# Expert layer: 1024 middle tokens routed into 23 sorted 128-row tiles run behind the recurrence, the other 1024 tokens dense in three chunks

## The reference

```python
xw = jnp.einsum('ntd,dh->nth', x, Wx) + b
def step(prev_h, xw_t):
    next_h = jnp.tanh(xw_t + prev_h @ Wh)          # 128 steps, one after the other
    return (next_h, next_h)
...
router_logits = jnp.einsum('bth,eh->bte', x, router_w)
topk_values, topk_indices = jax.lax.top_k(router_logits, TOP_K)      # TOP_K = 2 of 8
topk_weights = jax.nn.softmax(topk_values.astype(jnp.float32), axis=-1).astype(x.dtype)
h1 = jnp.einsum('bth,efh->btef', x, w1) + b1                          # f: 512
h1 = jax.nn.gelu(h1, approximate=False)
expert_outputs = jnp.einsum('btef,ehf->bteh', h1, w2) + b2
topk_expert_outputs = jnp.take_along_axis(expert_outputs, gather_idx, axis=2)
mixed_output = jnp.sum(topk_expert_outputs * topk_weights[..., None], axis=2)
...
x = x + _L1_ffn_ref(_L1_cond_ref(x, cond_1024, ...), ...)
```

## Time and profile before

| what | us |
|---|---|
| median of 3 runs (301.9 to 303.03) | 301.91 |
| profiled execution, from first to last instruction (its span) | 301.2 |
| PE busy | 264.4 (88%) |
| DVE busy | 258.8 (86%) |
| ACT busy | 215.6 (72%) |
| POOL busy | 76.2 (25%) |

### The profile page before, as it was taken

How to read it: one execution, slowest core, us unless ns; L and a number is a source line. 1 busy time by engine, 2 the same in 40 slices (tenths; PEclk the granted TensorE clock), 3 DMA queues, 4 the chain that set the end, 5 groups by cost and what they waited for, 6 DMA issues and landing times.

```text
span 301.2 us, 8834 instructions
## 1 busy us (share of the span) xinstructions
PE 264.4 (88%) x2716; PEld 205.5 (68%) x2716; DVE 258.8 (86%) x635; ACT 215.6 (72%) x455; POOL 76.2 (25%) x148
## 2 busy tenths in 40 slices
PE   4969940049989999999999999999999999999994
PEld 4824440016956777778888788888777887888874
DVE  4888999989898897779988799887799988889885
ACT  6367899998842677767777676667566766689892
POOL 3367997000025413011302112212110311101000
PEclk9989976557999999999999999999999999999999
DMA  6990443101500000000000000000001000001000
GB/s 186 314 310 4 84 94 76 28 0 35 90 17 2 0 3 1 0 2 2 19 0 0 2 3 26 2 0 0 1 2 30 8 0 0 2 1 37 0 2 27
DMA packets 24031, 10.63 MB, mean 35 GB/s; under 512 B 13355, under 2 KB 22982, under 8 KB 24006
## 3 DMA queue, kind: packets, MB, share of 16 engines
q1 hardware_dynamic: 23470, 10.05, 13.6%
q10 hardware_dynamic: 536, 0.26, 0.3%
HBM read 6.11 MB, written 1.05 MB: 24 GB/s over the span
## 4 chain that ended last, share of the span: by engine, by line
PE 79%; DVE 16%; issue 1%; ACT 1%; DMA 1%; SPq 0%; DVEq 0%
PE bank L893 78%; DVE peak L706 3%; DVE big L728 3%; DVE peak L633 2%; DVE big L711 1%; DVE big L744 1%; PE bank L937 1%; DMA y_sb<-in_cond 1%; PE bank L1017 0%; DVE big L746 0%; DVE wyT L779 0%; DVE pkm L626 0%; DVE big L738 0%; DVE x_sb L759 0%; DVE q L700 0%
## 5 line engine op out<-in xcount | busy, mean ns | idle before, releaser
L893 PE MATMUL bank<-big,wt 128*128 128x384 f16 (+2 forms) x480 | 124.8, 336 | 0.6 <-DVE big L872 0.5
L893 PE MATMUL bank<-wt,big 128*128 (+1 forms) x1536 | 111.5, 219 | 0.1
L872 DVE TENSOR_TENSOR big<-big 128x384 f16<-128x384 f32 (+2 forms) x160 | 93.2, 585 | 20.5 <-ACT big L594 16.1
L893 PEld LDWEIGHTS bank<-wt,big 128*128 128x128 f16 x1536 | 97.9, 97 | 16.2 <-issue 0.2
L592 ACT ACTIVATE big<-bank,miscT 128x384 f32<-128x384 f32 (+2 forms) x160 | 96.2, 602 | 15.3 <-PE bank L893 8.2
L893 PEld LDWEIGHTS bank<-q,wxh 128*128 128x128 f32 x254 | 44.4, 189 | 17.4 <-issue 3.4
L893 PEld LDWEIGHTS bank<-big,wt 128*128 (+1 forms) x480 | 50.0, 117 | 4.8 <-issue 1.1
L580 ACT ACTIVATE q<-bank (+1 forms) x112 | 20.6, 184 | 38.7 <-PE bank L893 37.9
L404 POOL CAST big<-q 128x64 f16<-128x64 f32 x32 | 13.2, 413 | 129.0 <-ACT q L580 126.5
L868 DVE CAST big<-big 128x512 f16<-128x512 f32 (+2 forms) x104 | 38.6, 372 | 4.8 <-ACT big L592 3.9
L827 DVE SCALAR_TENSOR_TENSOR wyT<-bank,gates,wyT 128x128 f32<-128x128 f32 x128 | 39.8, 343 | 1.0 <-issue 0.6
(11 more groups left out here) (165 smaller groups left out, 320.0 us busy)
## 6 DMA issues: line engine op xcount, KB each, us to landing
wnat<-in_w SPq DMA_DIRECT2D x8, 512.0 KB, 7.7
x_sb<-in_x SPq DMA_DIRECT2D x4, 256.0 KB, 4.3
out_block<-wyT SPq DMA_DIRECT2D x15, 64.0 KB
wn<-in_w_gate ACTq DMA_DIRECT2D x1, 192.0 KB, 4.9
wn<-in_w_up SPq DMA_DIRECT2D x1, 192.0 KB, 5.6
wn<-in_w_down SPq DMA_DIRECT2D x1, 192.0 KB, 5.7
b_in<-in_b SPq DMA_DIRECT2D x12, 4.0 KB
wt<-wyT SPq DMA_TRANSPOSE x8, 3.0
```

The source lines that it names most:

```text
L872: V.tensor_tensor(g_lo[:, par, f, 0:w], g32[:, f, 0:w], g_hi[:, par, f, 0:w], ALU.subtract).then_inc(g_lo_done, 1)
L893: return nc.tensor.matmul(o, l, r, start=start, stop=stop, skip_group_check=True)
```

## The change

The tokens are no longer all treated alike. Tokens 0 to 255, 256 to 767 and 1792 to 2047 are three dense chunks as before (256, 512 and 256 wide). The 1024 tokens from 768 to 1791 are **routed**: each token is put twice into a table in HBM (`xs_rows`), once for each of its two experts, sorted by expert, each expert's part rounded up to whole tiles of 128 rows. At most 2 x 8 + 7 = 23 tiles come of it, and 23 are always run.

- **Recurrence.** Chunk 0 (256 wide) carries one step in each slot, 32 in all; chunk 1 (512 wide, its four pairs now written out and not looped) carries two in each slot, 64 in all. The last 16 steps run by themselves in a new function `between`, ahead of chunk 2.
- **Routing.** `between` also makes the 1024 tokens' logits, their two best experts, each row's place (a cumulative count by matmuls with a triangle of ones, then some small DVE operations), copies of the tokens with tokens as rows (matmuls by the identity, eight ACT copies of 512 columns) and the table of tiles `m_tile` (expert and first row of each tile). The logits of chunk 2 wait for that table on PE.
- **Table.** SP writes 10112 rows of zeros (544 B each, 5.5 MB) to HBM behind the weight transposes, and two rows of `b2` behind that. POOL issues 16 indirect DMAs of 128 rows (`L588`), then splits chunk 2's gates.
- **Sparse tiles.** Behind chunk 2 each of the 23 tiles: SP reads its first row from `m_tile` into a register, loads the tile transposed from HBM and the rows' return addresses; PE reads the expert into a register and makes 12 hidden matmuls, and, two tiles later, one for the bias `b2` and 12 down matmuls, 128 columns each; ACT reads the expert too and makes four gelus; DVE makes high and low halves and takes the output from PSUM; POOL scatters it to a second table in HBM by an indirect DMA.
- **End.** When all 23 have landed, SP loads both rows of every token back, DVE adds them with their gates (16 operations), and the 8 tiles are stored.

```diff
-RNN_SLOTS = ((0, 1, 3, 4, 5, 7), range(8), range(8), (0, 1, 2, 4, 5, 6), ())
-RNN_FROM = [FIRST_STEPS + E // 2 * sum(len(n) for n in RNN_SLOTS[:c]) for c in range(CH)]
-HI_SCALAR = ((3,), (3,), (3,), (3,), (0, 1, 3))
+D_WIDTHS = (256, 512, 256)
+D_FROM = (0, 256, 1792)
+DCH = len(D_WIDTHS)
+D_TILES = [w // P for w in D_WIDTHS]
+D_BEFORE = [sum(D_TILES[:c]) for c in range(DCH + 1)]
+HI_SCALAR = ((3,), (), (0, 1, 3))
+RNN_PER_SLOT = (1, 2, 0)
+RNN_FROM = (FIRST_STEPS, FIRST_STEPS + 32, T - 16)
+RNN_REFILL = 32
+TAIL_STEPS = 16
+SP_FROM = 768
+SP = 1024
+SP_TILES = SP // P
+SP_TILE0 = SP_FROM // P
+NT = 2 * SP_TILES + E - 1
+XROW = 272
+XROWS = (E - 1) * SP + NT * P
+DUMP = NT * P
+YROWS = DUMP + 2 * SP
...
-        def chunks(eng, pair):
-            for c in range(CH):
-                pair(c, 0, c > 0)
-                with eng.Fori(1, E // 2 - (c == CH - 1)) as e2:
-                    pair(c, e2, True)
-            pair(CH - 1, E // 2 - 1, True)
+        def chunks(eng, pair, between):
+            pair(0, 0, False)
+            with eng.Fori(1, E // 2) as e2:
+                pair(0, e2, True)
+            for e2 in range(E // 2):
+                pair(1, e2, True)
+            between()
+            pair(2, 0, True)
+            with eng.Fori(1, E // 2 - 1) as e2:
+                pair(2, e2, True)
+            pair(2, E // 2 - 1, True)
...
-        def rnn_step(c, e2, s):
-            if s not in RNN_SLOTS[c]:
-                return None
-            return e2 * len(RNN_SLOTS[c]) + (RNN_FROM[c] + RNN_SLOTS[c].index(s))
-        def rnn_column(c, step):
-            return (step + -RNN_FROM[c]) * B
...
+        def rnn_steps(c, e2, s):
+            n = RNN_PER_SLOT[c]
+            return [e2 * (2 * NF * n) + (RNN_FROM[c] + n * s + i) for i in range(n)]
+        def rnn_column(c, e2, step):
+            return (step + -(RNN_FROM[c] + (RNN_REFILL if c == 1 and e2 >= 2 else 0))) * B
...
+            sp.wait_ge(s_consts, 1)
+            sp.dma_start(xs_rows.rearrange("(k p) r -> p k r", p=P),
+                         zrow[:, :].unsqueeze(1).to_broadcast([P, XROWS // P, XROW])).then_inc(xs_init, 16)
+            sp.wait_ge(b2r_zeroed, 1)
+            for row in (0, BH_LO):
+                sp.dma_start(b2r_in[row:row + 1, :], b2.rearrange("(a e) h -> a (e h)", a=1)).then_inc(ld_b2r, 16)
...
+            for i in range(2 * SP_TILES // 4):
+                sp.wait_ge(sent, 16 * 4 * (i + 1))
+            sp.wait_ge(m_done, 2)
+            for n in range(NT):
+                row = sp.value_load(m_tile[0:1, 1, n:n + 1], min_val=0, max_val=XROWS - P)
+                if n >= XBUF:
+                    sp.wait_ge(s_hid, NF * (n - XBUF + 1))
+                sp.dma_start_transpose(xs_in[:, n % XBUF, :, :], xs_rows[bass.ds(row, P), 0:2 * P]).then_inc(xs_ld[n % XBUF], 16)
+                if n >= 2 * XBUF:
+                    sp.wait_ge(spot_done, n - 2 * XBUF + 1)
+                sp.dma_start(back[:, 2 * n:2 * n + 2], xs_rows[bass.ds(row, P), 2 * P:2 * P + 2]).then_inc(
+                    back_ld[n % (2 * XBUF)], 16)
...
+            for i in range(4):
+                sp.wait_ge(y_sent[i], 16 * ((NT - i + 3) // 4))
+            back_rows = ys_rows[DUMP:YROWS, :].rearrange("(a j p) h -> p j a h", a=2, p=P)
+            for j in range(SP_TILES):
+                sp.dma_start(y_back[:, j, :, :], back_rows[:, j, :, :]).then_inc(y_in[j], 16)
+            for j in range(0, SP_TILES, 2):
+                sp.wait_ge(y_added, j + 1)
+                store(nc.sync, SP_TILE0 + j).then_inc(stored, 16)
...
+            for i in range(done, T // 4):
+                split_states(i)
+            pool.wait_ge(xs_init, 16)
+            pool.wait_ge(s_consts, 6)
+            pool.wait_ge(s_pos_done, 1)
+            for j in range(SP_TILES):
+                for a in range(2):
+                    pool.wait_ge(pay_done, j // 2 * 2 + a + 1)
+                    G.indirect_dma_start(out=xs_rows, out_offset=bass.IndirectOffsetOnAxis(ap=s_pos[:, a, j:j + 1], axis=0),
+                                         in_=payload[:, j, a, :], in_offset=None).then_inc(sent, 16)
+            split_gates(DCH - 1)
+            for n in range(NT):
+                pool.wait_ge(back_ld[n % (2 * XBUF)], 16 * (n // (2 * XBUF) + 1))
+                if n >= 4:
+                    pool.wait_ge(y_sent[n % 4], 16 * (n // 4))
+                G.tensor_scalar(spot[:, n % 4:n % 4 + 1], back[:, 2 * n:2 * n + 2].bitcast(F32), dump[:, n:n + 1], 0.0, ALU.max,
+                                ALU.add).then_inc(spot_done, 1)
+                pool.wait_ge(spot_done, n + 1)
+                pool.wait_ge(s_y_sb, n + 1)
+                G.indirect_dma_start(out=ys_rows, out_offset=bass.IndirectOffsetOnAxis(ap=spot[:, n % 4:n % 4 + 1].bitcast(U32), axis=0),
+                                     in_=y_st[:, n % 4, :], in_offset=None).then_inc(y_sent[n % 4], 16)
...
+            def take_payload(i):
+                j, a = i // 2 * 2, i % 2
+                act.wait_ge(pay_mm, j + 2)
+                A(payload[:, j:j + 2, a, 0:2 * P], banks[4 + j // 2][:, :].rearrange("p (j r) -> p j r", j=2),
+                  ACT.Copy).then_inc(pay_done, 1)
+            def between():
+                for k in range(TAIL_STEPS):
+                    step = T - TAIL_STEPS + k
+                    act.wait_ge(rnn_mm, step + 1)
+                    A(h32[:, step * B:(step + 1) * B], ps_rnn[:, k * B:(k + 1) * B], ACT.Tanh, scale=1 / WS).then_inc(h32_done, 1)
+                    if 5 <= k < 5 + SP_TILES:
...
+            for n in range(NT):
+                e = act.value_load(m_tile[0:1, 0, n:n + 1], min_val=0, max_val=E - 1)
+                for f in range(NF):
+                    act.wait_ge(s_hid, NF * n + f + 1)
+                    if n >= 2:
+                        act.wait_ge(s_lo, 2 * (n - 2) + f // 2 + 1)
+                    A(s_g32[:, n % 2, P * f:P * (f + 1)], hid_of(NF * n + f), ACT.Gelu,
+                      bias=miscT[:, bass.ds(e * NF + f, 1)], scale=1 / WS).then_inc(s_gelu, 1)
...
+            def take_y(n):
+                dve.wait_ge(s_y_mm, n + 1)
+                if n >= 4:
+                    dve.wait_ge(y_sent[n % 4], 16 * (n // 4))
+                V.tensor_copy(y_st[:, n % 4, :], ps_y[n % 2][:, 0:P]).then_inc(s_y_sb, 1)
+            for n in range(NT):
+                for half in range(2):
+                    dve.wait_ge(s_gelu, NF * n + 2 * half + 2)
+                    if n >= 3:
+                        dve.wait_ge(s_y_mm, n - 2)
+                    at = slice(2 * P * half, 2 * P * (half + 1))
+                    link(V.tensor_copy(s_ghi[:, n % 3, at], s_g32[:, n % 2, at]))
+                    V.tensor_tensor(s_glo[:, n % 3, at], s_g32[:, n % 2, at], s_ghi[:, n % 3, at], ALU.subtract).then_inc(s_lo, 1)
+                if n >= 3:
+                    take_y(n - 3)
+            for n in range(NT - 3, NT):
+                take_y(n)
+            dve.wait_ge(s_gate_done, 2)
+            for j in range(SP_TILES):
+                dve.wait_ge(y_in[j], 16)
+                a = acc[:, SP_TILE0 + j, :]
+                link(V.scalar_tensor_tensor(a, y_back[:, j, 0, :], s_gate[:, 0, j:j + 1], a, ALU.mult, ALU.add))
+                V.scalar_tensor_tensor(a, y_back[:, j, 1, :], s_gate[:, 1, j:j + 1], a, ALU.mult, ALU.add).then_inc(y_added, 1)
...
+                if c == DCH - 1:
+                    pe.wait_ge(m_done, 2)
...
+            def between():
+                pe.wait_ge(h32_done, T - TAIL_STEPS)
+                input_part(T - TAIL_STEPS, T)
+                for k in range(TAIL_STEPS):
+                    step = T - TAIL_STEPS + k
+                    pe.wait_ge(h32_done, step)
...
+            def sparse_up(n, e):
+                pe.wait_ge(xs_ld[n % XBUF], 16 * (n // XBUF + 1))
+                x_hi, x_lo = (xs_in[:, n % XBUF, low, :] for low in range(2))
+                for f in range(NF):
+                    w_hi, w_lo = (wt_flat[:, bass.ds(e * (4 * FF) + (low * FF + f * P), P)] for low in range(2))
+                    slot = NF * n + f
+                    if slot == HID_BANKS.index(3):
+                        pe.wait_ge(b2_added, DCH)
+                    if slot >= len(HID_BANKS):
+                        pe.wait_ge(s_gelu, slot - len(HID_BANKS) + 1)
+                    o = hid_of(slot)
+                    mm(o, w_hi, x_hi, True)
+                    mm(o, w_lo, x_hi, False)
+                    mm(o, w_hi, x_lo, False).then_inc(s_hid, 1)
+            def sparse_down(n, e):
+                if n < 2:
+                    pe.wait_ge(added, LATE + E * D_BEFORE[DCH])
+                else:
+                    pe.wait_ge(s_y_sb, n - 1)
+                o = ps_y[n % 2][:, 0:P]
+                mm(o, ones[:, 0:P], b2_rows[:, bass.ds(e * P, P)], True)
+                for f in range(NF):
+                    w_hi, w_lo = (wt_flat[:, bass.ds(e * (4 * FF) + (2 * FF + low * FF + f * P), P)] for low in range(2))
```

(17 more changed lines are left out.)

327 lines of the change are left out of this document (247 added, 80 removed).

## The result

The changed kernel takes 326.41 us (median of 4 runs, 325.08 to 328.33) where the kernel before takes 302.0 us (4 runs): a ratio of 1.079, 95% interval 1.076 to 1.083. It is slower, as forecast, by 24.4 us in place of the 18 forecast. Its profiled execution has a span of 325.0 us. The kernel before was run again beside each set of experiments, with medians from 302.0 to 302.8 us; a ratio is to the runs of its own set, and a difference in us across sets is uncertain by about 0.8.

The account below looks back on a forecast made before the run. PE's matmuls were taken to bound the kernel; about 93 us of pairs leave, 23 sparse tiles paced by PE's sequencer come. Terms from chunk 0's logits at 103.5 sum to 319.3, plus 0.7: 320.0 us, range 303 to 343.

Parts of the forecast that it names:

- Chunk 0: First dense chunk, 256 wide: 30.7 us before plus 2.9 for 8 more recurrence steps, 33.6, ending at 137.1.
- Zeroing the table: SP's 5.5 MB zeroing, with POOL waiting for the `b2` rows behind it: costs nothing unless the rate is under 110 GB/s.
- Chunk 1: 512-wide chunk, modelled on the earlier chunk 2 (47.5 us) plus 32 steps, second refill and a wait: 53.7, ending at 190.8.
- the recurrence can't take two steps a slot: Rival for chunk 1: slots take 2.03 us, not 1.65, 12 us more, 332; chance 0.07.
- Between: Lone steps at 0.67 us, refill, logits, copies, last state and wait for the table of tiles: 17.3 us, ending at 208.1.
- Chunk 2: Last dense chunk, 256 wide, no steps: ACT sets 0.825 us a slot; 26.0 us with last down products, ending at 234.1.
- Sparse tiles: 23 tiles behind chunk 2, paced by PE's sequencer (computed addresses, register load) at 3.1 us each: 71.3 us, ending at 305.4.
- address work costs nothing: Rival for sparse tiles: PE's address work runs ahead, DVE paces at 1.8 us a tile, 41 for 71.3, 290; chance 0.10.
- The register load is dear: Rival for sparse tiles: a load costs near a DMA's 1.7 us, PE 4.2 a tile, 25 us more, 345; chance 0.13.
- SP 2.4: SP's work per sparse tile: load 0.6, transpose 1.23 and DMA 0.60, 2.4 us, under PE's 3.1.
- The late scatters: Rival in chunk 2: POOL's 16 scatters run slow, gates come 8 us late, 328, or 337 if casts block them; chance 0.13.
- The end: After the last matmul: copy, scatter, landing, eight loads, additions and last store, 13.9 us where 3.7 remained before.

Follow-up runs that it names:

- the kernels with constants: Changed kernel with sparse tiles' weight addresses constant on PE: 319.69 us, ratio 1.056; with ACT's bias and SP's rows constant too: 301.26 us, ratio 0.997.
- the rows come later: Changed kernel with POOL's clearing, loading and splitting of the `b2` rows moved behind chunk 1's gates: 322.2 us, ratio 1.063.
- the kernel with the loads ahead: Changed kernel with `b2` rows later, chunks 0 and 2 written out, PE's and SP's register loads made before the sparse tiles: 303.15 us, ratio 1.002.

## Why the prediction was right, and where it was off

The forecast was 320.0 us, slower, with PE's sequencer as the cause. The time is 326.4, inside the range, and the cause is shown by the kernels with constants. Behind the largest term, which held, smaller errors cancelled. Term by term, in the profiled execution, whose span is 1.4 us under the median where the sum allowed 0.7:

| term | forecast | measured | ends at |
|---|---|---|---|
| up to chunk 0's logits | 103.5 | 104.3 | 104.3 |
| chunk 0 | 33.6 | 38.6 | 143.0 |
| chunk 1 | 53.7 | 50.5 | 193.5 |
| between | 17.3 | 17.6 | 211.1 |
| chunk 2 | 26.0 | 27.0 | 238.1 |
| sparse tiles | 71.3 | 71.0 | 309.1 |
| end | 13.9 | 15.9 | 325.0 |

**Chunk 0** is the mis-sized term, and the step that failed in it is the sentence under "Zeroing the table": POOL's work on the `b2` rows was priced by what POOL itself is late for, at nothing. It blocks DVE, which was on the path in the first pair: 3.5 us. I had quoted the Trainium skill on the shared ports, but only for the case in which DVE locks POOL out; the same section ("SBUF — State Buffer", "SBUF: two separate sides") says it for the other direction. Of the 0.8 us ahead of the chunk 0.5 go with it (103.8 where the rows come later): the `memset` of the rows, 0.95 from 102.87, stands beside a cast that took 0.82 where it takes 0.28. (Across all the traces this mark stands between 101.9 and 104.3, so the other 0.3 says nothing.) The rest, 35.1 - 33.6 = 1.5, is mostly the price of a slot with a step in the loop: I had 1.085, and eight slots of the changed kernel's loop take 9.13 us (122.92 to 132.05), 1.14 each, which for 24 slots is 1.3 more.

**Chunk 1** came in 3.2 us shorter. Its slots are 1.65 us apart as summed, but the sum counted two slots too many. Its model, chunk 2 of before, was measured from logits to logits, and the copy of the logits comes when the third slot begins: two slots of the next chunk are in the 47.5. Here the chunk ends where the refill for the lone steps begins (193.53), and from the copy at 142.96 only 30 slots remain: 53.7 - 2 x 1.65 = 50.4. The second refill left no gap: PE is busy 50.50 of 50.50 us. With that, the rival that the recurrence can't take two steps a slot is false.

**Between** held to 0.3 us, but by luck. A lone step took 0.67 us as summed only at first (PE in order of time):

```profile
194.65 0.40 PE L1149 MATMUL bank<-q,wxh 128*128 128x16 f32 x2 [0.27 <-ACT q L772]
195.32 0.40 PE L1149 MATMUL bank<-q,wxh 128*128 128x16 f32 x2 [0.27 <-ACT q L772]
...
205.57 0.59 PE L1149 MATMUL bank<-q,wxh 128*128 128x16 f32 x2
206.43 0.61 PE L1149 MATMUL bank<-q,wxh 128*128 128x16 f32 x2 [0.27 <-ACT q L772]
```

Once PE was down to single steps with a wait in each, its granted clock fell to 0.50 (1.2 GHz) at about 197.8 and stayed there until about 214.9. From 198.5 on a step takes 0.88, with one of ACT's copies behind its tanh or without: the last one above has none and takes 0.86. So the 0.2 a copy of the sum, 1.6 us, is wrong, the copies fit beside PE's part of the step, and some 1.9 us of slower clock, of which the sum had nothing, stand in its place. PE waited 0.83 us for the table (`m_tile`, L1105) where 1.8 was in the sum.

**Chunk 2** came within 1.0 us, by luck too. Its first slots ran at the lower clock: from the logits to the slot at 215.31, 2.4 slots took 4.2 us. The slot at 211.87 took 1.92 us, where a slot with the same products, with the clock at 1.00 (the kernel with the loads ahead, 201.31), took 0.99. The other 28 took 20.0 us, 0.72 each and not 0.825, since ACT doesn't set the pace. The 0.825 added up durations, but ACT's gelus overlap too (ACT in order of time):

```profile
228.22 0.47 ACT L750 ACTIVATE big<-bank,miscT 128x256 f32<-128x256 f32 x1
228.58 0.48 ACT L752 ACTIVATE big<-bank,miscT 128x256 f16<-128x256 f32 x1
```

They start 0.36 apart, so seven of them take 2.5 us in four slots, 0.63 a slot, under PE's 0.66; PE was busy 5.00 of 5.00 us from 225 to 230. Behind the last slot 2.7 us pass until the first tile, where the sum had 1.7: the last down products, and 0.57 of "issue" ahead of the first tile.

**Sparse tiles**: 3.05 us against 3.1. The load was entered as 0.6 + 0.2 and costs 0.7 to 0.8, of which the load itself is 0.31 and the rest the gaps; the addresses 2.3 against 2.2. The rival "address work costs nothing" is false, and of the next limit it is half right: without register work the pace is 1.97, not far from its 1.8, but with POOL's queue nearest to a limit and not DVE, and the time 301, not 290. "The register load is dear" is false: 0.31 where 1.7 was feared, and the gaps make it 0.8. "SP 2.4" was wrong, 2.77, without effect on the time, as PE was later still.

**The late scatters** did not come true, by 0.7 us: a scatter is 0.97 at best and 1.27 at most beside DVE's work in chunk 2, and one that ran across a cast (the cast at 224.18, the scatter from 223.75) took 0.97. The wait of 2.5 that the forecast took from the Trainium skill's example isn't seen in any of the 16. The same section of the Trainium skill ("SBUF: two separate sides") ends the block with the VectorE instruction. A cast here is 0.29 us long, so the example's length should not have been carried over. The same ports did their damage elsewhere.

**The end** took 2.0 us more. The last tiles have no up products between them, so their y comes faster than POOL can scatter it (POOL, in order of time):

```profile
307.04 1.06 POOL L599 DMA_INDIRECT ys_rows<-wnat,spot  x1 [1.39 <-DVE wnat L1124]
...
312.06 1.05 POOL L599 DMA_INDIRECT ys_rows<-wnat,spot  x1 [0.28 <-POOL spot L595]
```

The last y is copied by 309.4 and its scatter starts at 312.06, behind two others 1.67 apart in POOL's queue. The sum had let it start at once. These 2.7 us of backlog, less 0.7 by which the other terms of the end came in shorter, are the 2.0; that is read from the trace, and no kernel was made to try it.

The balance of the change: 64 pairs of tile and expert, 93 us by the forecast's rate, leave; 71 us of sparse tiles come, and with the lone steps, a narrow chunk whose first slots run at the lower clock and the way back through memory the saving is gone before chunk 0's 5 us.

## What to carry to other kernels

Price a step on an idle engine also by whom it shares something with: a POOL instruction of 1 to 2 us can cost a cast or a two-input instruction of DVE beside it nearly its whole length, so it belongs where DVE has slack. When work becomes small per address (128 columns a matmul), count the addresses and register loads of PE's queue, not the columns: here 2.3 us of address work and 0.8 of load stand against 1.6 us in which the array does the same products without them. Loads into registers can go ahead, to a stretch with room for them, if they are done by the time their engine is needed: SP's 23 took 14 us, and PE then waited 1.8 us for its first tile. A short loop over narrow tiles (256 columns here) was worth writing out, one over 384 columns or more was not. And take an engine's pace from the distance between starts, not from durations, on ACT as on PE.

## What the runs showed of the hardware

- A POOL instruction can hold DVE's casts and two-input instructions up until it ends: 0.29 became 2.02 us, 0.15 became 0.99, beside POOL's TENSOR_TENSOR on a single partition (2.11 us) and TENSOR_SCALAR on 33 (1.09 us); few partitions didn't help.
- A register load from SBUF takes 0.28 us on SP and 0.31 on PE. With the check and the register work behind it SP made one every 0.6 us, and from its start until PE multiplied again it was 1.0, of which the array stood idle for 0.6 to 0.8.
- A scatter of 128 rows by indirect DMA holds POOL for 0.97 us (544-byte rows) or 1.06 (512-byte rows), with 0.3 to the next, and lands 2.4 to 2.5 us from issue (medians; 3.5 at most). A transposing DMA holds SP's queue for 1.2 us.
- The granted clock fell from 1.00 to 0.50 (2.4 to 1.2 GHz) behind stalls of 0.82 and 1.33 us in chunk 0's first pair, for about 3.4 us, and in the stretch of lone steps with waits of 0.27, for 17 us. At 0.50 a lone step took 0.88 us where it took 0.67, and a slot of chunk 2 with 15 matmuls 1.92 where it took 0.99.
